# Two attention and two expert layers on one core: score banks divided two and four, the last gathers issued back to back, the last batch combined in halves

## The reference, cut to what matters

```python
x = L0_attn_a_x                                   # (8, 512, 128) f32
x = x + attn_a(layernorm(x), W_attn, b_attn, W_proj, b_proj)   # 16 heads of 8, RoPE, causal softmax
x = x + ffn(layernorm(x), expert_sel, keys, values)
x = x + attn_b(layernorm(x), WQ, WK, WV)          # one head of 128, band of 64, softmax over all
x = x + ffn(layernorm(x), expert_sel, keys, values)

def ffn(x, expert_sel, keys, values):             # 64 experts of size 128, top 4 of them
    sel = sigmoid(x @ expert_sel.T)
    sel_val, sel_idx = top_k(sel, 4)
    gates = zeros(N, 64).at[arange(N)[:, None], sel_idx].set(sel_val)
    h = einsum('nd,kde->nke', x, keys)
    return einsum('nke,kev->nv', relu(h) * gates[:, :, None], values)
```

## Time and profile before

| | us |
|---|---|
| median of three runs | 1338.33 (1334.89 to 1345.9) |
| the profiled execution, time | 1334.34 |
| the profiled execution, span | 1332.4 |
| PE busy | 877.1 (66%) |
| PEld busy | 601.8 (45%) |
| DVE busy | 808.2 (61%) |
| ACT busy | 484.9 (36%) |
| POOL busy | 836.1 (63%) |
| granted TensorE clock, mean | 0.806 |

### The profile page before, as it was taken

How to read it: one execution, slowest core, us unless ns; L and a number is a source line. 1 busy time by engine, 2 the same in 40 slices (tenths; PEclk the granted TensorE clock), 3 DMA queues, 4 the chain that set the end, 5 groups by cost and what they waited for, 6 DMA issues and landing times.

```text
span 1332.4 us, 20381 instructions
## 1 busy us (share of the span) xinstructions
PE 877.1 (66%) x6298; PEld 601.8 (45%) x6298; DVE 808.2 (61%) x2325; ACT 484.9 (36%) x1249; POOL 836.1 (63%) x1023
## 2 busy tenths in 40 slices
PE   1999988988899658798776453423288756964100
PEld 0334433333344227798675332313177756864100
DVE  2677888798887424664674874635586752653212
ACT  1156646565455513364443211101134323542000
POOL 5234647879766766287982647556367473996575
PEclk9999989999898858898897665555678887987655
DMA  6555533332261334587563101012125544863321
GB/s 191 200 193 198 190 125 119 97 94 95 70 213 54 90 104 118 153 243 223 165 168 91 45 28 51 35 37 84 31 72 163 153 143 121 239 182 114 100 68 53
DMA packets 206537, 163.67 MB, mean 123 GB/s; under 512 B 15968, under 2 KB 191072, under 8 KB 206432
## 3 DMA queue, kind: packets, MB, share of 16 engines
q1 hardware_dynamic: 185696, 112.00, 29.3%
q0 software_dynamic: 16384, 33.59, 7.9%
q10 hardware_dynamic: 4352, 16.78, 3.3%
HBM read 78.94 MB, written 83.36 MB: 122 GB/s over the span
## 4 chain that ended last, share of the span: by engine, by line
PE 34%; DVE 30%; POOL 14%; issue 11%; another core or an unknown queue 6%; DMA 2%; SPq 2%; ACT 1%; POOLq 0%; DVEq 0%; ACTq 0%
POOL v_aug L1621 8%; PE ps L697 6%; PE ps L706 5%; PE ps L600 5%; PE ps L538 4%; DVE x_res L1322 3%; PE ps L579 3%; PE ps L686 3%; PE ps L565 3%; DVE row_max L1096 2%; POOL w_attn L1604 2%; DVE st L1040 1%; DVE block_max L1096 1%; DVE dest_f L1291 1%
## 5 line engine op out<-in xcount | busy, mean ns | idle before, releaser
L1608 POOL DMA_INDIRECT sorted_rows<-xn,dest x256 | 253.2, 989 | 166.6 <-DVE dest L1295 107.2
L1621 POOL DMA_INDIRECT v_aug<-result_rows,dest x256 | 245.5, 959 | 132.1 <-issue 64.9
L883 ACT ACTIVATE arena<-ps 128x512 f32<-128x512 f32 x320 | 182.7, 605 | 105.9 <-PE ps L538 98.0
L697 PE MATMUL ps<-arena 128*128 128x128 f32 x1024 | 153.8, 299 | 54.8 <-DVE arena L1307 30.8
L565 PE MATMUL ps<-arena 64*128 64x128 bf16 (+3 forms) x576 | 142.8, 311 | 39.9 <-DMA arena<-k_parts 16.9
L872 ACT COPY arena<-ps 128x512 f32<-128x512 f32 x128 | 75.0, 586 | 254.3 <-PE ps L706 160.9
L697 PEld LDWEIGHTS ps<-arena 128*128 128x128 f32 x1024 | 140.1, 212 | 60.7 <-DVE arena L1307 32.9
L1307 DVE COPY arena<-ps 128x512 f32<-128x512 f32 x128 | 88.1, 689 | 125.6 <-PE ps L686 77.0
L706 PE MATMUL ps<-arena 128*128 x1024 | 148.2, 292 | 18.0 <-ACT arena L872 7.7
L1096 DVE TENSOR_REDUCE row_max<-ps 128x1 f32<-128x512 f32 (+1 forms) x192 | 128.9, 684 | 42.5 <-PE ps L579 39.8
L706 PEld LDWEIGHTS ps<-arena 128*128 128x128 f32 x1024 | 136.7, 208 | 20.0 <-issue 19.9
(11 more groups left out here) (190 smaller groups left out, 1302.9 us busy)
## 6 DMA issues: line engine op xcount, KB each, us to landing
arena<-sorted_rows SPq DMA_DIRECT2D x128, 256.0 KB
result_rows<-arena SPq DMA_DIRECT2D x128, 256.0 KB
sorted_rows<-arena ACTq DMA_DIRECT2D x16, 1024.0 KB, 4.4
arena<-q_parts SPq DMA_DIRECT2D x16, 512.0 KB
arena<-k_parts SPq DMA_DIRECT2D x16, 512.0 KB
q_parts<-parts SPq DMA_DIRECT2D x52, 128.0 KB, 2.8
k_parts<-parts SPq DMA_DIRECT2D x50, 128.0 KB, 2.9
sorted_rows<-xn,dest POOLq DMA_INDIRECT x256
```

The costliest lines, as they stand in the source:

```text
L697: mm = pe.matmul(ps[:, e_bank(2, layer, half, n), P * i:P * i + P], ktile[:, v, P * i:P * i + P], xtt[:, v, P * i:P * i + P], start=True, ...
L883: nc.scalar.activation(prob[:, grp % 2, pr % 2, PROB_AT[u]:PROB_AT[u] + T], ps[:, v % 3, :], ACT.Exp, scale=SCALE_A).then_inc(exp_done, 1)
L1608: g.indirect_dma_start(sorted_d[b // HALF][:, :], bass.IndirectOffsetOnAxis(dest[:, 16 * b + n:16 * b + n + 1], 0), xn1[:, b % 2, n // TOP ...
L1621: g.indirect_dma_start(yg[:, b % 2, i // TOPK, C * c:C * c + C], None, result_d[layer][b // HALF][:, :], bass.IndirectOffsetOnAxis(dest[:, ...
```

## The change

Four things are edited. In attention a the exponentials' scores get two PSUM banks (0 and 1) and the maxima's scores four (2 to 5). In the last expert half only two combines stand between the steps, batch 0 behind step 13 and batch 1 behind step 26; batches 2 to 6 are combined after all steps. None of the second layer's eight gathers is paced. The last batch is gathered on two semaphores, eight DMAs each, and combined and written out in two halves of two tiles.

```diff
-COMBINE_AT = (12, 19, 26, 33)
+COMBINE_AT = (13, 26)
...
+        yg_last = sem("yg_last")
...
-            for b in range(B):
-                sp.wait_ge(combined, 16 * (B + b + 1))
-                sp.dma_start(out_d.rearrange("(t p) c -> p t c", p=P)[:, TT * b:TT * b + TT, :],
-                             x[:, TT * b:TT * b + TT, :]).then_inc(done_out, 16)
-            sp.wait_ge(done_out, 16 * B)
+            for half in range(2 * B):
+                if half % 2 or half >= 2 * B - 2:
+                    lo = TT * (half // 2) if half < 2 * B - 2 else 2 * half
+                    sp.wait_ge(combined, 16 * B + 8 * (half + 1))
+                    sp.dma_start(out_d.rearrange("(t p) c -> p t c", p=P)[:, lo:2 * half + 2, :], x[:, lo:2 * half + 2, :]).then_inc(done_out, 16)
+            sp.wait_ge(done_out, 16 * (B + 1))
...
# scores_kq
-                if v >= 3:
-                    pe.wait_ge(exp_done, v - 2)
+                if v >= 2:
+                    pe.wait_ge(exp_done, v - 1)
-                    return pe.matmul(ps[:, v % 3, at:at + n], ...
+                    return pe.matmul(ps[:, v % 2, at:at + n], ...
# scores_qk
-                if n >= 3:
-                    pe.wait_ge(s1_free, n - 2)
-                bank = ps[:, 3 + n % 3, :]
+                if n >= 4:
+                    pe.wait_ge(s1_free, n - 3)
+                bank = ps[:, 2 + n % 4, :]
# the exponentials read ps[:, v % 2, :], the maxima ps[:, 2 + n % 4, :]
...
+            def combine_part(part):
+                b = B - 1
+                n = B + b
+                if part:
+                    dve.wait_ge(yg_last, 128)
+                else:
+                    dve.wait_ge(yg_in[b % 2], 256 * (n // 2) + 128)
+                for c in range(TOPK):
+                    dve.wait_ge(combined, 16 * n + 8 * part + 2 * c)
+                    for t in (2 * part, 2 * part + 1):
+                        xt = x[:, TT * b + t, :]
+                        nc.vector.scalar_tensor_tensor(out=xt, in0=yg[:, b % 2, t, C * c:C * c + C],
+                                                       scalar=top[:, TT * b + t, c:c + 1], in1=xt,
+                                                       op0=ALU.mult, op1=ALU.add).then_inc(combined, 1)
...
-            for b in range(HALF, B):
+            for b in range(len(COMBINE_AT), B - 1):
                 combine(1, b)
+            for part in range(2):
+                combine_part(part)
...
# gather
-                    c = i % TOPK
+                    c, late = i % TOPK, (layer, b) == (1, B - 1) and i >= TT * TOPK // 2
...
+                                         ).then_inc(yg_last if late else yg_in[b % 2], 16)
...
             for b in range(B):
-                gather(1, b, paced=b < HALF - 1)
+                gather(1, b, paced=False)
```

More of the change, by code:

```diff
@@ L532, in scores_kq @@
                 v = 5 * pr + u
-                if v >= 3:
-                    pe.wait_ge(exp_done, v - 2)
+                if v >= 2:
+                    pe.wait_ge(exp_done, v - 1)
                 def block(hb, pair, j, at):
                     rows, n = slice(64 * hb, 64 * hb + 64), T - P * j
-                    return pe.matmul(ps[:, v % 3, at:at + n], kk[rows, s, pair, P * j:P * j + P], qs[rows, s, pair, P * j:T],
+                    return pe.matmul(ps[:, v % 2, at:at + n], kk[rows, s, pair, P * j:P * j + P], qs[rows, s, pair, P * j:T],
                                      start=True, stop=True)
@@ L882, in _ @@
                         act.wait_ge(s2_ready, v + 1)
-                        nc.scalar.activation(prob[:, grp % 2, pr % 2, PROB_AT[u]:PROB_AT[u] + T], ps[:, v % 3, :], ACT.Exp,
+                        nc.scalar.activation(prob[:, grp % 2, pr % 2, PROB_AT[u]:PROB_AT[u] + T], ps[:, v % 2, :], ACT.Exp,
                                              scale=SCALE_A).then_inc(exp_done, 1)
@@ L1619, in gather @@
                 for i in range(lo, hi):
-                    c = i % TOPK
+                    c, late = i % TOPK, (layer, b) == (1, B - 1) and i >= TT * TOPK // 2
                     g.indirect_dma_start(yg[:, b % 2, i // TOPK, C * c:C * c + C], None, result_d[layer][b // HALF][:, :],
-                                         bass.IndirectOffsetOnAxis(dest[:, 16 * b + i:16 * b + i + 1], 0)).then_inc(yg_in[b % 2], 16)
+                                         bass.IndirectOffsetOnAxis(dest[:, 16 * b + i:16 * b + i + 1], 0)
+                                         ).then_inc(yg_last if late else yg_in[b % 2], 16)
                     if paced:
```

## The result

The changed kernel took **1375.52 us** (median of 4 runs, 1371.56 to 1380.46) against 1336.61 for the kernel before, measured beside it: ratio 1.0282, 95% interval 1.0251 to 1.0313, slower. The forecast was 1354, with a range of 1320 to 1370. The profiled execution took 1372.9 us with a span of 1371.2, against 1334.34 and 1332.4 before, so the spans differ by 38.8 us.

A forecast was written before the change was run, and what follows sets the result against it. The prediction took the last result copy of the expert steps, which releases batch 4's gather, to set the end. +28.6 - 2.3 - 8 = +18.3 made 1334.34 into 1352.6; adjusted toward the median, 1354 us, range 1320 to 1370.

The forecast's parts named there:

- banks: Attention a: fewer waits for maxima (ceiling 22.8 us) less more for exponentials (at most 17 us), taken as -8 us.
- steps: Last expert half: last result copy, and so batch 4's gather, 28.6 us later through steps disturbed beside unpaced gathers.
- tail: End of the last layer: halving the last combine takes off 2.3 us; the extra write counted as nothing, bound 0.5.
- The walk: Last expert half followed step by step: 2.22 us a step, 0.7 of exposed time lost, last result copy at 1266.8.
- the third rival: Heavy disturbance: first two gather batches let almost no step pass, adding 8 to 12 us or more; 1362 to 1372, chance 0.08.
- the combine of batch 2: Start of batch 4: a new wait ending about 1269.5, tying with the results written at 1269.9.
- tied to indirect DMAs issued back to back: Expert steps and banded attention: engines held up beside unpaced indirect DMAs; lost share 0.71 for scatters, 0.72 for the gather.
- the mild: Expert steps: a lost share of 0.35, 30 us lost instead of 60; 1323 to 1327 us, chance 0.17.
- rival 1: Expert steps: no disturbance, 2.22 us each beside unpaced gathers, batch 4 starts 30.7 us earlier; 1293 us, chance 0.13.

The follow-up runs named there:

- e1: The kernel before with only the banks of attention a changed (two for exponentials, four for maxima), stalling chip: 1357.34 us, ratio 1.0059.
- e11: The kernel before with two banks for the exponentials and still three for the maxima, free chip: 1233.19 us, ratio 1.0076.
- e3: The changed kernel with the memsets back in the gathers of batches 0 to 2, stalling chip: 1338.64 us, ratio 0.9921.
- e4: The changed kernel with banks three and three and gathers of batches 0 to 2 paced, stalling chip: 1335.25 us, ratio 0.9898.
- e13: The changed kernel unaltered, timed again on another stalling chip: 1387.36 us, ratio 1.0314 to the kernel before.
- e5: e2 plus a 128x16 memset between the DMAs of batches 0 to 2, stalling chip: 1386.63 us, ratio 1.0291 to the kernel before.
- e17: e4 with the memset also between all indirect DMAs of the banded attention and the last scatters, free chip: 1279.19 us, ratio 1.0426.
- e15: e5 with the memset lengthened to 128x320 (DMAs 1.50 us apart), stalling chip: 1364.38 us, ratio 1.0133 to the kernel before.
- e2: The changed kernel with the banks put back to three and three, stalling chip: 1387.55 us, ratio 1.0292 to the kernel before.
- e7: e2 with each indirect DMA of batches 0 to 2 fetching 128 pieces of 128 B instead of 512 B: 1384.98 us, ratio 1.0274.
- e6: e2 with GpSimd waiting after each four indirect DMAs of batches 0 to 2 until all landed: 1355.37 us, ratio 1.0076.
- e8: The kernel before with only the pacing of batches 0 to 2 in the second layer removed, stalling chip: 1387.35 us, ratio 1.0290.
- e16: The changed kernel unaltered, timed on a free chip: 1210.54 us, ratio 0.9887 to the kernel before.
- e14: e4 timed again on another stalling chip: 1337.46 us, ratio 0.9911 to the kernel before.

## Why the prediction was wrong

It was 20.3 us too low for the profiled execution (1352.6 against 1372.9), and the terms account for it: banks 14.9, steps 4.6, tail 1.0, rounding -0.2. (Half of 4.0 added to 1352.6 is 1354.6, so 1354 was a little low too.)

*The step that failed is the banks of attention a, -8.* The pair of traces has +6.9, and timed alone the banks cost 0.6% (e1). The gain's mechanism was right (waits for maxima 22.8 to 6.4), but two sizes were not. The loss: I took a fifth of its 17 us because the slots in question "are those in which TensorE would next stand for VectorE". e11 measures that part alone at 0.8%, some 9 us, half of the ceiling, though on a free chip. The gain: I took half of 22.8 us; e1 less e11 leaves 2 or 3 of it, which their intervals don't tell from nothing. That there is no gain of 8 us is firm. How large the loss is, is not: e3 against e4 and e13 against e5 put it at 0.2%. The 6.9 is read at the first gather of the last stage, which the nine traces with three and three banks on stalling chips reach anywhere from 1121.5 to 1142.2 us. At the end of attention a the same nine have their last exponential at 478.7 to 485.2, 482.0 in the mean, and the four with two and four banks at 480.2 to 489.7, 485.2 in the mean: a loss of about 3 us, with ranges that overlap.

*The clock* I left out altogether. In the stretch of 200 to 300 us it is 0.87 to 0.90 in all seven traces with two banks for the exponentials, and 0.95 in eleven of the thirteen with three. But e17, with three, has 0.92, and e15, also with three, has 0.88:

```profile
200.00:300.00 100.00, 89.42 (x689) 38.79 (x689) 81.91 (x201) 56.66 (x106) 75.11 (x99) 0.88 0.30 95
```

Its last exponential still ends at 481.5, within the range above. Over 90 to 440 us the two kinds overlap: 0.91 to 0.94 with three banks, 0.89 to 0.92 with two. So two banks and a lower clock in this window go together, but that the one brings the other, and what it costs, is not shown.

*The expert steps, +28.6:* 33.2. The walk's form held throughout: three stands of GpSimd over 13 us (32.66, 27.11, 14.02), combines 0 and 1 without a wait, steps at 2.22 us between the disturbances. One term was mis-sized: of the 40.8 us exposed beside batches 0 and 1, 0.87 were lost and not 0.7. That was the third rival's mechanism, two batches on end letting almost nothing pass, with 6.7 us instead of its 8 to 12. The two single batches lost 13.3 and 14.0 where I had 15.6 each. At batch 4 the results decided, and not the combine of batch 2 that GpSimd's row names: the last result copy ends at 1278.28, and the gather starts 3.1 us later, as in the kernel before, while the combine of batch 2 is done at about 1280.3, and batches 2 and 3 started 0.3 us after the combine that they had waited for. That copy ends 7.4 us after step 31 instead of 5.6. Timed apart, this term looks worse: e2, without the banks, costs 40.7 us (34 to 44) where my terms for the same parts give 26.3. Its trace loses 36.9 us between the first gather and batch 4 (156.4 against 119.6 in e1, same chip), so on that chip the steps were too low by some 8 us. The banks and the steps both were too small; how much falls to each differs with the pair of runs.

*The cause, "tied to indirect DMAs issued back to back",* was right in effect and wrong in word. Something between them does not help (e5); fewer bytes don't (e7); a longer interval does, by degrees, with a memset (e15, e4) or without (e6). The stall goes with the rate at which they are issued. e8 shows that nothing else in the change is needed for it. The Trainium skill's page "SBUF — State Buffer", section "SBUF: two separate sides", says that engine and DMA ports can't contend with one another. The free chip behaves so (e16). The stalling ones don't speak against it either: VectorE's and ScalarE's instructions keep their lengths, and it is their start that comes late (ScalarE stood 28.09 us). What holds the starts up is not settled: the profile says remote, and no run here could look behind it.

*The tail, -2.3:* -1.3. Both halves take 2.57 us as reckoned, 2.1 less than the 4.66 for what comes last. But from the end of the last combine to the end of the span it is 3.4 us instead of 2.8, with one more write out, and I had bounded that at 0.5.

*Chances and range.* I gave the mild and the absent disturbance 0.30 together against 0.08 for the heavy one, and spread the banks only from -16 to +6, though I had bounded them at +17. With +7 for the banks the same walk gives 1367.6, and 1369.6 with the 2 us added for the median, just inside the range. The direction came right because the chip of the result was of the kind that my rows came from: on the free chip where it was timed (e16) the change is 1.1% faster, which is rival 1, at 0.13.

## What to carry to other kernels

A stand that the profile calls remote beside indirect DMAs is a question of their rate: pace them where other engines work beside them, not in the tail, and time the pacing on more than one chip, because here it was worth 3 to 4% on one kind and cost about 1% on the other. A bank moved from one user to another takes a wait away from one place and puts it in many small ones, so price the loser's side from its own ceiling. One pair of traces can't size such a term: kernels with the same code up to the first gather of the last stage reached it up to 10 us apart on one and the same chip (1131.9 us in e6, 1142.2 in e14). An instruction put in as a spacer must lengthen the interval in the timeline, or it spaces nothing.

## What was unexpected of the hardware

- Chips of the same type differ: the kernel before takes 1337 to 1347 us on some and 1225 on others, and the remote waits (36 with 256.4 us in one trace) are absent on the latter.
- The stall goes with the interval of indirect DMAs: 1.77 us none, 1.50 us steps at about half their speed, 1.26 us stands of up to 28 us. In a stand VectorE's instructions keep their length of 0.69 us; a relu started 14.7 us after the matmuls that it needed. The stall does not depend on whether each moves 128 rows of 512 or of 128 bytes.
- GpSimd needs 0.95 us for an indirect DMA and about 0.30 until the next; a memset of 0.13 us fits into these 0.30 for nothing.
- The granted clock of a stretch can differ between traces of kernels with the same code there: over 200 to 300 us, with three and three banks, 0.95 in eleven traces, 0.92 in one and 0.88 in one.
